# A decoder layer on one core: the scaling of attention rows moved to VectorE, the cross-attention's query weights multiplied into the keys, and loads waited for in two parts

## What is computed

```python
# self-attention, 16 heads of 64, with a positional term that depends on the logits
q, k, v = to_heads(x @ Wq), to_heads(k), to_heads(v)          # k, v = split(x @ Wkv)
sim = einsum('bid,bjd->bij', q, k) * scale
sim = sim + _cope(q, sim, pos_emb)       # suffix sums of sigmoid(sim), cut at 63, interpolated table
out = softmax(sim) @ v                    # then @ Wout + b_out
x = layernorm(x + out)
# cross-attention, one head of 256
Q = query @ Wq + bq;  K = key_value @ Wk + bk;  V = key_value @ Wv + bv
x = layernorm(x + softmax(Q @ K.T) @ V @ Wo + bo)
# low-rank FFN
x = layernorm(x + gelu(x @ U1 @ V1 + b1) @ U2 @ V2 + b2)
```

## Time and profile before

| | |
|---|---|
| time, median of 3 runs | 2276.32 us (2276.25 to 2277.36) |
| profiled execution | 2276.31 us, span of the instructions 2274.5 us |
| TensorE busy | 2187.8 us (96%) |
| ScalarE busy | 1750.6 us (77%) |
| VectorE busy | 1634.1 us (72%) |
| GpSimd busy | 389.3 us (17%) |
| attention, up to the last scaling | about 1841 us |
| cross stage | 1847 to 2274 us |
| granted TensorE clock, mean | 0.992 |

### The profile page before, as it was taken

The page is one execution under the profiler, slowest core; times in us unless marked ns, Lnnn a source line. Parts: engine busy times, 40 slices in busy tenths (PEclk is TensorE's granted clock), DMA queues, the critical chain, the costliest instruction groups (busy, mean ns, idle before and its releaser), DMA issues. The chain is left out here.

```text
span 2274.5 us, 53491 instructions
## 1 busy us (share of the span) xinstructions
PE 2187.8 (96%) x14577; PEld 1484.5 (65%) x14577; DVE 1634.1 (72%) x4269; ACT 1750.6 (77%) x3723; POOL 389.3 (17%) x673
## 2 busy tenths in 40 slices
PE   7999999999999999999999999999998979999997
PEld 5666666666666666666666666666665547777775
DVE  5888888888888888888888888888888811323232
ACT  5888888888888888888888888888888843454543
POOL 1111111111111111111111111111111101212121
PEclk9999999999999999999999999999999989999998
DMA  2010101010101010101010101010101031010100
GB/s 68 24 30 24 30 23 30 24 30 24 32 24 32 25 30 24 31 24 30 24 30 24 30 24 30 24 31 24 27 15 48 11 67 35 30 39 30 39 30 7
DMA packets 107088, 67.05 MB, mean 29 GB/s; under 512 B 27821, under 2 KB 104814, under 8 KB 106990
## 3 DMA queue, kind: packets, MB, share of 16 engines
q1 hardware_dynamic: 106990, 65.56, 10.9%
HBM read 14.33 MB, written 2.10 MB: 7 GB/s over the span
## 5 line engine op out<-in xcount | busy, mean ns | idle before, releaser
L845 DVE TENSOR_REDUCE mx<-Sc 128x1 f32<-128x1024 f32 (+1 forms) x512 | 564.8, 1128 | 216.2 <-PE Sc L634 216.2
L484 ACT ACTIVATE probsT<-rings 128x512 f32<-128x512 f32 x1024 | 542.1, 601 | 172.8 <-PE rings L642 172.8
L508 ACT ACTIVATE probs<-Sc,nbias 128x1024 f32<-128x1024 f32 x512 | 568.3, 1124 | 28.1 <-DVE nbias L855 28.1
L642 PEld LDWEIGHTS rings<-ident,probs 128*128 128x128 f32 x4096 | 446.5, 143 | 203.5 <-issue 114.5
L642 PE MATMUL rings<-ident,probs 128*128 128x128 f32 x4096 | 529.7, 277 | 2.2 <-ACT probs L508 2.2
L634 PE MATMUL Sc<-qk,q_now 64*128 64x512 f32 x2048 | 507.3, 607 | 16.7 <-ACT qk L419 6.1
L656 PE MATMUL out<-probsT,V 128*64 128x256 f32 x4096 | 498.3, 384 | 18.9 <-issue 9.7
L656 PEld LDWEIGHTS out<-probsT,V 128*64 128x64 f32 x4096 | 311.7, 136 | 140.5 <-issue 66.0
L808 DVE COPY_PREDICATED z<-mask,z 128x224 f32<-128x224 int16 (+5 forms) x768 | 394.6, 514 | 11.3
L376 POOL TENSOR_TENSOR prod<-cut,z 128x350 f32<-128x350 f32 x128 | 120.4, 941 | 1452.4 <-DVE z L820 1452.4
L634 PEld LDWEIGHTS Sc<-qk,q_now 64*128 64x128 f32 x2048 | 181.0, 186 | 177.8 <-issue 162.0
(11 more groups left out here) (128 smaller groups left out, 2288.4 us busy)
## 6 DMA issues: line engine op xcount, KB each, us to landing
q_now<-qk SPq DMA_DIRECT2D x256, 64.0 KB, 2.0
xv<-xT SPq DMA_DIRECT2D x113, 128.0 KB, 2.2
q_far<-qk SPq DMA_DIRECT2D x256, 32.0 KB, 1.8
at<-attn SPq DMA_DIRECT2D x16, 512.0 KB, 3.2
probs<-in_x_dram SPq DMA_DIRECT2D x4, 512.0 KB, 5.6
wqk<-in_L_attn_Wq_dram SPq DMA_DIRECT2D x32, 64.0 KB, 2.0
xin<-in_x_dram SPq DMA_DIRECT2D x16, 128.0 KB, 2.8
out_dram<-res SPq DMA_DIRECT2D x16, 128.0 KB, 1.7
```

The costliest lines, as they stand in the source:

```text
L484: nc.scalar.activation(probsT[:, u, 4 * s:4 * s + 4, :], ring[SLOT_BANK[k]][:, :].rearrange("p (t q) -> p t q", q=P), ACT.Copy).then_inc(s ...
L508: nc.scalar.activation(probs[:, u, cols], Sc[:, cols], ACT.Exp, bias=nbias[:, u:u + 1], accum_out=sums[:, u, half:half + 1]).then_inc(exp_ ...
L642: last = nc.tensor.transpose(ring[SLOT_BANK[k]][:, j * P:(j + 1) * P], probs[:, u, (4 * s + j) * P:(4 * s + j + 1) * P], ident[:, :])
L845: nc.vector.tensor_reduce(mx[:, u, half:half + 1], Sc[:, cols], AX.X, ALU.max).then_inc(dve_unit, 1)
```

## The change

It has four parts. In attention the turns stand two sets of transposes earlier in TensorE's order, and the scaling of the turned rows goes from ScalarE to VectorE, behind the bias of u = 0. In the cross stage the query's weights are multiplied into the keys once: Wqk = Wk Wq^T is made by TensorE from transposed weights, bq times Wk becomes a bias of the keys, and the scores take the normalised x1 in place of the query. Because a normalised row sums to zero, its last column is replaced by ones (x1q), the last row of Wq is subtracted from the others (WqR, by VectorE), and bq takes the free place. QT's slots, matmuls and evacuations go from each tile, and x1T moves behind qT. The loads of Wq2 and bq go to the early ones (EARLY = 8). The rest is waited for in two parts: values_in (Wv2, Wo2, bv, now issued first) ahead of the product of Wv and Wo, and loaded (LOADS = 18) ahead of the first tile.

```diff
-EARLY = 5
+EARLY = 8
...
     eng.dma_start(parts["Wk2"], A["L0_xattn_Wk"].rearrange("(c p) n -> p c n", p=P)).then_inc(loaded, 16)
+    eng.dma_start(A["Wq2"][:, :, :], A["L0_xattn_Wq"].rearrange("(c p) n -> p c n", p=P)).then_inc(loaded, 16)
     for k in range(DC):
         eng.dma_start(parts["bk"][:, k:k + 1],
                       A["L0_xattn_bk"][k * P:(k + 1) * P].rearrange("(p a) -> p a", a=1)).then_inc(loaded, 16)
+        eng.dma_start(A["bq"][:, k:k + 1],
+                      A["L0_xattn_bq"][k * P:(k + 1) * P].rearrange("(p a) -> p a", a=1)).then_inc(loaded, 16)
 
 
 def attention(nc, A):
@@ -485,15 +488,6 @@
                                          ring[SLOT_BANK[k]][:, :].rearrange("p (t q) -> p t q", q=P),
                                          ACT.Copy).then_inc(slot_out, 1)
 
-            def scale(g, u):
-
-                h, t = g // PAIRS, g % PAIRS
-                if u == 0:
-                    act.wait_ge(rsum_done, g + 1)
-                    wait_apart(act, turned, g + 1, waited)
-                nc.scalar.activation(attn[:, t * 2 + u, bass.ds(h * C, C)], turns[:, u * C:(u + 1) * C], ACT.Copy,
-                                     scale=rsum[:, u:u + 1]).then_inc(scaled, 1)
...
                     transposed(0, base, at.late, (2, 3))
-                    transposed(1, base, at.last, (0, 1))
-                    if not second:
-                        scale(g - 2, 0)
-                        scale(g - 2, 1)
-                    transposed(1, base, at.last, (2, 3))
+                    transposed(1, base, at.last)
...
             transposed(0, base, at.late, (2, 3))
-            transposed(1, base, at.last, (0, 1))
-            scale(G - 2, 0)
-            scale(G - 2, 1)
-            transposed(1, base, at.last, (2, 3))
+            transposed(1, base, at.last)
             empty_halves(G - 1)
-            scale(G - 1, 0)
-            scale(G - 1, 1)
 
...
                 if not first:
                     transposes(0, base, at.late, 2, late_before)
                     transposes(0, base, at.late, 3, late_before)
+                    if not second:
+                        turns_of(g - 2)
                     transposes(1, base, at.last, 0, late_before)
                     transposes(1, base, at.last, 1)
-                    if not second:
-                        turns_of(g - 2)
                     transposes(1, base, at.last, 2)
                     transposes(1, base, at.last, 3)
                     outputs(g - 1, base, at.last, range(EARLY_TILES), keys, empty=not second)
...
             transposes(0, base, at.late, 3, late_before)
+            turns_of(G - 2)
             transposes(1, base, at.last, 0, late_before)
             transposes(1, base, at.last, 1)
-            turns_of(G - 2)
...
+            def scale(g):
+
+                h, t = g // PAIRS, g % PAIRS
+                wait_apart(dve, rsum_done, g + 1, waited)
+                wait_apart(dve, turned, g + 1, waited)
+                for u in range(2):
+                    nc.vector.tensor_scalar(attn[:, t * 2 + u, bass.ds(h * C, C)], turns[:, u * C:(u + 1) * C],
+                                            rsum[:, u:u + 1], None, ALU.mult).then_inc(scaled, 1)
...
                 bias(g, 0)
+                if not (first or second):
+                    scale(g - 2)
                 if chain:
                     first_shifts(c)
                 half_max(g, 1, 0)
@@ -907,9 +903,10 @@
...
-            dve.wait_ge(rsum_done, G - 1)
+            scale(G - 2)
             add_halves(G - 1)
             invert(G - 1)
+            scale(G - 1)
...
 
         loaded = sem("loaded")
-        LOADS = 24
...
 
         ORDER = [("atT0", "X"), ("atT1", "X"), ("x2T", "Z"), ("prT0", "Y"), ("prT1", "Y"),
-                 ("pT", "Z"), ("prT2", "Y"), ("prT3", "Y"), ("h0", "Z"), ("h1", "Z"), ("x1T", "X"),
-                 ("qT", "Z"), ("QT0", "X"), ("QT1", "X")]
+                 ("pT", "Z"), ("prT2", "Y"), ("prT3", "Y"), ("h0", "Z"), ("h1", "Z"), ("qT", "Z"),
+                 ("x1T", "X")]
         MISC = [("Wout", "X"), ("V2", "Z")]
         NORM = [("x2", "Z"), ("x1", "X"), ("x3", "Z")]
 
...
 
-        FUSED = 4 * len(MB)
...
-            for dst, name in ((Wv2, "L0_xattn_Wv"), (Wout, "L0_attn_Wout"),
-                              (Wq2, "L0_xattn_Wq"), (Wo2, "L0_xattn_Wo"), (U1, "L0_ffn_U1"), (U2, "L0_ffn_U2")):
+            for dst, name in ((Wv2, "L0_xattn_Wv"), (Wo2, "L0_xattn_Wo")):
+                sp.dma_start(dst[:, :, :], A[name].rearrange("(c p) n -> p c n", p=P)).then_inc(values_in, 16)
+            sp.dma_start(bv[:, :], A["L0_xattn_bv"].rearrange("(a n) -> a n", a=1).broadcast_to([P, D]))\
+                .then_inc(values_in, 16)
...
+
+            empty(0, WqT[:, :, :], square, par=0)
+            empty(1, WkT[:, :, :], square, par=1)
+            n = 2
             for c in range(DC):
                 for lo, w in MB:
                     empty(n, cxT[:, c, lo:lo + w], lambda r: r[:, 0:w], par=n % 2)
                     n += 1
+                if c == 0:
+                    empty(n, Wqk[:, :, :], square, par=n % 2)
+                    empty(n + 1, bqk[:, :], lambda r: r[:, 0:DC], par=(n + 1) % 2)
+                    n += 2
             for c in range(DC):
                 for lo, w in MB:
-                    empty(n, K2T[:, c, lo:lo + w], lambda r: r[:, 0:w], ACT.Identity, par=n % 2, bias=bk[:, c:c + 1])
+                    empty(n, K2T[:, c, lo:lo + w], lambda r: r[:, 0:w], ACT.Identity, par=n % 2,
+                          bias=bqk[:, c:c + 1])
                     n += 1
             empty(n, WvT[:, :, :], lambda r: r[:, :].rearrange("p (c n) -> p c n", n=D), par=n % 2)
             empty(n + 1, bvT[:, :, :], lambda r: r[:, 0:DC * P].rearrange("p (c n) -> p c n", n=P), par=(n + 1) % 2)
...
-                if "X" in stages:
-                    out_of("x1T", x1T[:, :, :], chunks)
                 if "Z" in stages:
                     out_of("qT", qT[:, :], lambda r: r[:, 0:P])
                 if "X" in stages:
-                    for c in range(DC):
-                        out_of(f"QT{c}", QT[:, c, :], lambda r: r[:, 0:P], ACT.Identity, bias=bq[:, c:c + 1])
+                    out_of("x1T", x1T[:, :, :], chunks)
 
             act.wait_ge(loaded, LOADS * 16)
             body(-1, "X", rest=False)
...
             def done(last):
                 last.then_inc(slot_full, 1)
 
+            for n, W in enumerate((Wq2, Wk2)):
+                for e in range(DC):
+                    for c in range(DC):
+                        last = nc.tensor.transpose(ring[n][:, e * D + c * P:e * D + (c + 1) * P],
+                                                   W[:, c, e * P:(e + 1) * P], ident[:, :])
+                done(last)
+            n = 2
             for c in range(DC):
                 for b, (lo, w) in enumerate(MB):
-                    if n >= 2:
-                        pe.wait_ge(slot_out, n - 1)
+                    pe.wait_ge(slot_out, n - 1)
                     for j in range((w + P - 1) // P):
                         rows = min(P, w - j * P)
                         last = nc.tensor.transpose(ring[n % 2][:, j * P:j * P + rows],
                                                    cx[0:rows, 4 * b + j, c * P:(c + 1) * P], ident[0:rows, 0:rows])
                     done(last)
                     n += 1
-            pe.wait_ge(slot_out, 2 * len(MB))
+                if c == 0:
+                    pe.wait_ge(keyed, DC + 1)
+                    pe.wait_ge(slot_out, n - 1)
+                    for k in range(DC):
+                        for e in range(DC):
+                            last = nc.tensor.matmul(ring[n % 2][:, k * D:(k + 1) * D], WkT[:, e, k * P:(k + 1) * P],
+                                                    WqR[:, e, :], start=e == 0, stop=e == DC - 1)
+                    done(last)
+                    pe.wait_ge(slot_out, n)
+                    for k in range(DC):
+                        for e in range(DC):
+                            last = nc.tensor.matmul(ring[(n + 1) % 2][:, k:k + 1], WqR[:, e, k * P:(k + 1) * P],
+                                                    bk[:, e:e + 1], start=e == 0, stop=e == DC - 1)
+                    done(last)
+                    n += 2
+            pe.wait_ge(slot_out, n)
             for c in range(DC):
                 for lo, w in MB:
                     pe.wait_ge(slot_out, n - 1)
                     for k in range(DC):
-                        last = nc.tensor.matmul(ring[n % 2][:, 0:w], Wk2[:, k, c * P:(c + 1) * P],
+                        last = nc.tensor.matmul(ring[n % 2][:, 0:w], Wqk[:, k, c * P:(c + 1) * P],
                                                 cxT[:, k, lo:lo + w], start=k == 0, stop=k == DC - 1)
                     done(last)
...
-                        last = nc.tensor.matmul(Sc[:, lo:lo + w], QT[:, c, :], K2T[:, c, lo:lo + w],
```

(23 more changed lines are left out.)

34 lines of the change are left out of this document (22 added, 12 removed).

## The result

The changed kernel takes 2236.89 us (median, 2236.02 to 2237.25) where the kernel before takes 2276.84 beside it: a ratio of 0.9824, 95% interval 0.9808 to 0.9839, so 40 us or 1.8% faster. The forecast was 2238.

A forecast was written before the change was run, and what follows sets the result against it. TensorE was taken to set the pace, with a short wait for the scaling hidden in its busy time. Loop 23, early loads -1.2, start +0.6 and tiles +16.1 gave 38.5 us off 2276.3: 2238 us, range 2228 to 2258.

The forecast's parts named there:

- Loop: Attention: TensorE's output loads wait for the scaling; removing it wins 0.18 to 0.19 us a unit, 23 us over 126 units.
- Why the scaling was late: Attention: ScalarE reaches the scaling late because it empties four banks first, 2.06 us.
- VectorE's pair: Attention: two scalings on VectorE take 0.6 us, done at 1007.2; idle before second maxima falls from 1.55 to 0.76.
- Banks: Attention's transposes: sixth set up to 0.1 us late for its bank, fourth set wins about as much; net 0.
- Rival 3: Attention: VectorE's pair delays the mask chain, slower from 1.36 us; 2293 us at 1.8 us for the pair; chance 0.04.
- Early loads: Attention, unit 120: three more DMAs ahead of its queries cost 1.2 us once, bounds 0.8 to 2.3.
- Start: Cross stage's start: load wait and low clock give up to 5.4 us, added work costs 4.8; net gain 0.6.
- Tile: Cross stage: scores start 0.92 us earlier in 14 full tiles, 1.62 in two without FFN; 16.1 us in all.
- rival 2: Cross stage: VectorE's sum, norm and maxima hide half or all of the tile gain; 2244 or 2251 us; chance 0.12.

The follow-up runs named there:

- e1: Kernel before with only the attention loop's part: turns earlier, scaling on VectorE; cross stage and its loads as before. 2248.51 us.
- e3: Changed kernel with the scaling back on ScalarE between the halves of the last sets, turns still early. 2282.73 us.
- e4: Changed kernel with the turns back at their old place, VectorE still scaling. 2271.64 us.
- e8: Changed kernel with VectorE's scaling three steps later, behind the sixth mask, even shift and fifth mask. 2245.28 us.
- e5: Changed kernel with the scaling on ScalarE, ahead of all evacuations of the last sets, turns still early. 2278.89 us.
- e7: Changed kernel with six copies of zeros, which feed nothing, added on VectorE behind its scaling in every unit. 2272.00 us.
- e11: Changed kernel with three copies of zeros, which feed nothing, added on VectorE behind its scaling in every unit. 2238.16 us.
- e2: Kernel before with only the cross-stage part: folded query weights, three more early loads, loads waited for in two parts. 2263.82 us.
- e12: Changed kernel with TensorE waiting for all later loads at its first wait, not for the values' three alone. 2237.74 us.
- e10: Changed kernel with each tile's V2 pass moved behind the first scores of the next tile. 2243.56 us.
- e9: Changed kernel with the early cross-attention loads issued behind unit 120's far queries, not ahead of them. 2233.89 us.
- e6: Changed kernel with x1's transposes back ahead of the U2 passes, and ScalarE's evacuations alike. 2240.17 us.

## Why the prediction held, step by step

- **Loop, 23 us predicted, 27.9 measured (e1).** That TensorE's outputs wait for the scaling is shown from both sides: the wait goes with the change and comes back in e3, e4 and e8. The term was mis-sized: 0.18 to 0.19 a unit was read from the loads' idle alone, and the period fell by 0.225, 0.196 of it ahead of the outputs and 0.029 in their 24 loads.
- **Why the scaling was late.** The prediction put it down to ScalarE's four evacuations and had the turns done 0.6 us after their first load. They are read 1.05 us after it at the earliest (e5), so before the change the turns themselves ended last, 0.04 us behind the evacuations. By that they are ready 0.1 to 0.2 us ahead of the end of VectorE's first bias in the changed kernel, not 0.7. The plan worked since it moved both.
- **VectorE's pair, 0.6 us.** It takes 0.51 us, plus 0.40 of standing ahead. The first mask starts 0.83 us behind the bias's end, where it started 0.06 ahead of it, so the chain is delayed by 0.89; idle before the second maxima is 0.56, predicted 0.76. The end at 1005.76 against 1005.9 needed leaves 0.1 to 0.2, not the 0.4 of the prediction; e8 measures 0.13.
- **Banks, net 0.** Right in its result: in the changed kernel no transposes wait for a bank; e5 shows the price when they do. But the fourth set, said to wait for a bank before the change, didn't: the idle between the unit's transposes is 0.05 us in both kernels.
- **Rival 3, the pair too long.** Its threshold was a delay of 1.36 us. The pair delays the chain by 0.89, and the slack above that is 0.65 (e7, e11), so the threshold is 1.54.
- **Early loads, 1.2 lost.** The stall grew from 1.42 to 2.66, by 1.24, in the changed kernel's profile, where the clock stays at 1.00. In eight of the ten other profiles with these loads the granted clock falls behind the stall, and the unit is longer than its run's median by 3.8 to 5.6 us, where it was 1.5 before the change. That is 2.4 to 4.2 us lost, outside the bound of 2.3, and the prediction had no term for it. e2's unit ran 2.7 us over that of before, half of it idle.
- **Start, 0.6 won.** Measured 1.4 won: up to the first key loads +3.3 (predicted 4.8), the wait -3.0, the low clock -1.7 (predicted 2.0). The gain was ascribed to the loads; e12 shows that the added work took the wait's place, and the split of the waits did nothing.
- **Tile, 0.92 won.** Measured 0.73 in a full tile and 0.92 in the last, 10.4 in all, and 1.6 at each of the two places without FFN: 13.6 for 16.1. The failed part: scores "at x1T's end" overlooked V2's passes, which stand between. From U2's first load the prediction has the scores after 1.95 us; it is 2.12 here and 1.94 in e10, where V2 stands behind them. VectorE's idle before the last maxima is 0.63, not 0.24, so rival 2 is out; e10 shows a cover behind it too.
- **Tail, not predicted.** From the last scores to the end 42.3 us, 40.9 before.

What the page on VectorE says against the move (the Trainium skill, VectorE: DVE Perf Modes, Specifications: ScalarE nearer to PSUM) made no difference here: the pair takes 0.51 us on VectorE and 0.52 on ScalarE. The Trainium skill's formula (VectorE: DVE Perf Modes, the section on the TRN2 errata) gave 0.38 us for the pair, an estimate that the measured 0.51 replaces. On the queues (the Trainium skill, DMA: Bandwidth & Descriptors, Queues, rings and completion order) e9 agrees with the ring's order: the same loads behind the queries cost nothing there.

That the sum came within 1.1 us of the time is in part luck, since errors cancel: the loop 4.9 better, tiles 2.5 worse, start 0.8 better, tail 1.4 worse.

## What to carry to other kernels

When a result is late, look at both what it waits for and the queue it stands in: here the turns' place and ScalarE's queue ended within 0.04 us of each other, and moving one alone made the loop slower. Before a job is given to another engine, measure that engine's slack by adding work until the time moves; under the slack it was free here, above it the excess counted once in each of some 125 units. Where a small load is urgent, a large one is better issued right behind it than ahead of it.

## What the runs showed of the hardware

- Ahead of its pair VectorE stands 0.40 us where two address computations follow a short instruction (the changed kernel's loop). It stands 0.08 where there is nothing to compute (the last two units) and 0.08 behind three queued instructions (e8).
- Two copies of VectorE (128x176) that are recorded at 0.25 us each start 0.16 us apart: the sum of durations overstates the added time by half.
- The granted clock in the tail. Ahead of the last tile's transposes TensorE idles 2.36 us before the change, and its clock stays at 1.00 (2.4 GHz); after it idles 2.60 us, the stretch behind is granted 0.72 on the mean, part of it at 1.2 GHz, and eight transposes take 1.57 us instead of 0.86:

```profile
2241.74 0.86 PEld L1615 LDWEIGHTS ring<-ident,pr 128*128 128x128 f32 x8 [2.36 <-ACT pr L1478]
2240.00:2246.00 6.00, 4.01 (x29) 3.38 (x30) 0.06 (x1) 4.85 (x8) 0.00 (x0) 1.00 0.00 0
```

```profile
2200.27 1.57 PEld L1646 LDWEIGHTS ring<-ident,pr 128*128 128x128 f32 x8 [2.60 <-ACT pr L1493]
2198.00:2204.00 6.00, 3.73 (x22) 3.07 (x23) 0.55 (x3) 3.34 (x5) 0.00 (x0) 0.72 0.00 0
```

The first two rows are of the kernel before, the others of the one after. Of the tail's 1.4 us 0.24 is the longer idle and 1.1 the slower stretch behind it. All twelve profiles with the changed cross stage have this (idle of 2.58 to 2.95 us, the transposes in 1.04 to 1.57), the two with the old one (before, e1) don't.
- The length of the idle alone does not decide it. Ahead of the last unit's transposes every profile has an idle of 2.67 us. Behind it the clock stays at 1.00 in nine of fourteen, among them those of both kernels, and falls in five; these rows are of the kernel after and of e9:

```profile
1805.58 0.86 PEld L627 LDWEIGHTS rings<-ident,probs 128*128 128x128 f32 x8 [2.67 <-ACT probs L502]
```

```profile
1803.85 1.57 PEld L627 LDWEIGHTS rings<-ident,probs 128*128 128x128 f32 x8 [2.67 <-ACT probs L502]
```

What does decide it stays open. No run changed an idle on its own.
- Behind the 2.1 MB of early loads the same unit takes 16.5 to 19.4 us in executions of kernels that are alike up to there (the changed kernel, e6, e10, e12). The idle itself varies by 0.4 us (2.66 to 3.08); the rest goes with the clock behind it, and one profile doesn't size it.
